# Perceiver layer on one core: context loads released by the copies of a buffer, a layer norm in 10 steps instead of 12, and re-derived instruction orders

## The reference

```
x = x + xattn(layernorm(x), context)   # second layer norm with gamma/beta, 16 heads of 64, mask over the 257 keys
x = x + attn(layernorm(x))             # self attention over the 32 tokens, 16 heads of 16
x = x + ffn(layernorm(x))              # sigmoid(xr Wr^T) * (relu(xk Wk^T)^2 Wv^T), xr/xk mix a token with the one before
```

## Time and profile before

| | us |
|---|---|
| median of 3 runs | 874.78 (873.36 to 875.11) |
| the profiled execution | 873.3 |
| span of its profile, first to last instruction | 870.3 |
| PE busy | 812.6 (93%) |
| DVE busy | 611.1 (70%) |
| ACT busy | 600.3 (69%) |
| POOL busy | 423.7 (49%) |
| mean granted TensorE clock | 0.988 of 2.4 GHz |

### The profile page before, as it was taken

How to read it: one execution, slowest core, us unless ns; L and a number is a source line. 1 busy time by engine, 2 the same in 40 slices (tenths; PEclk the granted TensorE clock), 3 DMA queues, 4 the chain that set the end, 5 groups by cost and what they waited for, 6 DMA issues and landing times.

```text
span 870.3 us, 20253 instructions
## 1 busy us (share of the span) xinstructions
PE 812.6 (93%) x7355; PEld 669.2 (77%) x7355; DVE 611.1 (70%) x1871; ACT 600.3 (69%) x1423; POOL 423.7 (49%) x664
## 2 busy tenths in 40 slices
PE   8779999999999989999999989999999989888886
PEld 7568669896788858896788868896788857677664
DVE  4744575879577884879567884879668874767375
ACT  2659876798477875799567975799567875667422
POOL 1155524665437534766337533766337534656211
PEclk9899999999999999999999999999999999999999
DMA  8311010010101020011101120110100110010000
GB/s 236 109 25 37 26 50 13 25 26 26 50 26 26 25 62 13 26 27 25 50 18 29 29 62 14 26 26 25 50 14 26 36 51 10 17 26 1 26 2 12
DMA packets 49521, 30.50 MB, mean 35 GB/s; under 512 B 22928, under 2 KB 48336, under 8 KB 49424
## 3 DMA queue, kind: packets, MB, share of 16 engines
q1 hardware_dynamic: 48528, 29.12, 12.3%
q10 hardware_dynamic: 896, 0.10, 0.1%
HBM read 26.85 MB, written 2.10 MB: 33 GB/s over the span
## 4 chain that ended last, share of the span: by engine, by line
PE 74%; DVE 12%; ACT 8%; issue 4%; SPq 1%; POOL 1%; DMA 0%; POOLq 0%; ACTq 0%; DVEq 0%
PE score L780 16%; PE pre L665 6%; PE post L866 6%; PE probT L791 5%; DVE qk_t L1281 4%; PE post L875 3%; PE aux L724 3%; PE ac_main L806 3%; PE ac_tail L808 2%; PE ac_main L807 2%; PE ac_tail L812 2%; PE ac_main L811 2%; DVE qk_l L1276 2%; PE post L846 2%; PE post L884 2%
## 5 line engine op out<-in xcount | busy, mean ns | idle before, releaser
L430 POOL TENSOR_TENSOR prT_l<-prT,prT_h 128x512 fp32r<-128x512 f32 x128 | 164.5, 1290 | 173.0 <-ACT prT_h L1070 172.8
L564 POOL TENSOR_SCALAR pr<-pr,rsum,poison 128x257 f32<-128x257 f32 x256 | 148.8, 593 | 138.0 <-DVE rsum L1305 137.0
L1299 DVE CUSTOM_DVE_ANT_0 sm<-score,mbias 128x257 f32<-128x257 f32 x256 | 106.5, 420 | 92.6 <-PE score L780 78.8
L1051 ACT ACTIVATE pr<-sm,nmx 128x257 f32<-128x257 f32 x256 | 128.8, 505 | 42.9 <-DVE nmx L1299 37.5
L780 PE MATMUL score<-cT_h,qk_h 128*128 128x258 f32 x256 | 91.6, 358 | 6.2 <-DVE qk_t L1281 4.7
L1059 ACT ACTIVATE prT<-probT 128x512 f32<-128x512 f32 x128 | 75.6, 591 | 30.0 <-PE probT L791 28.2
L791 PE MATMUL probT<-ident,pr 128*128 128x128 f32 x512 | 78.8, 277 | 9.3 <-ACT prT L1059 7.0
L1070 ACT ACTIVATE prT_h<-prT 128x512 fp32r<-128x512 f32 x128 | 80.2, 627 | 8.2 <-PE ac_tail L812 7.4
L791 PEld LDWEIGHTS probT<-ident,pr 128*128 128x128 f32 x512 | 60.3, 142 | 19.5 <-issue 7.1
L780 PE MATMUL score<-cT_h,qk_t 128*128 128x258 f32 x256 | 73.7, 288 | 0.0
L780 PE MATMUL score<-cT_h,qk_l 128*128 128x258 f32 x256 | 73.4, 287 | 0.0
(11 more groups left out here) (336 smaller groups left out, 2195.6 us busy)
## 6 DMA issues: line engine op xcount, KB each, us to landing
cx_in<-in_ctx_dram SPq DMA_DIRECT2D x64, 192.0 KB, 2.4
cx_in<-in_ctx_dram SPq DMA_DIRECT2D x64, 64.0 KB, 2.3
xn<-in_x_dram SPq DMA_DIRECT2D x8, 256.0 KB, 3.2
xb<-in_x_dram SPq DMA_DIRECT2D x8, 256.0 KB, 3.3
out_dram<-yo SPq DMA_DIRECT2D x7, 256.0 KB, 3.0
wq<-in_L_xattn_Wq_dram SPq DMA_DIRECT2D x2, 512.0 KB, 7.8
wo<-in_L_xattn_Wo_dram SPq DMA_DIRECT2D x1, 1024.0 KB, 8.2
wqkv<-in_L_attn_W_qkv_dram SPq DMA_DIRECT2D x1, 768.0 KB, 8.7
```

What stands on the lines that cost most here:

```text
L430: eng.tensor_tensor(prT_l[:, :, cut], prT[:, :, cut], prT_h[:, :, cut], ALU.subtract).then_inc(prob_lower, 1)
L564: last = pool.tensor_scalar(p, p, rsum[:, j % 2, t:t + 1], poison[:, 0:1], ALU.mult, ALU.mult)
L1051: act.activation(pr[j % 2][:, t, :], sm[:, t % 2, :], ACT.Exp, bias=nmx[:, j % 2, t:t + 1], scale=-1.0, accum_out=ssum[:, j % 2, t:t + 1]) ...
L1299: dve.tensor_tensor_reduce(sm[:, t % 2, :], score[t % 2][:, 0:NK], mbias[:], DH ** -0.5, BIG, ALU.add, ALU.min, nmx[:, j % 2, t:t + 1]).th ...
```

## The change

1. SP waits for `c_lower` (DVE's `CL`, which itself comes after ACT's `CU`, which comes after PE's `CT`) before it loads a buffer anew, and no longer for `ac_done`. In group 0 `spread_last_values()` comes behind the loads of batches 4 and 5 instead of ahead of them.
2. The layer norm has 10 steps. The seed is taken straight from the bits of the negative w by one instruction, so the shift step is gone; the polynomial of the first round is of a higher order (steps 4, 5, 6), followed by one round (7, 8), in which w2 = -1.6875 (scale var + shift) stands for w; step 9 applies. The integer tile `li` is gone.
3. The lists: the names for steps 10 and 11 of `A`, `B` and `C` are dropped in `DVE_ORDER` and `DVE_LAST`. In `DVE_FIRST`, besides, `S2:1 S3:1` go behind `A3` to `A8`, `CL:1` and `R0:1`, and `A9`, now the application, comes before `R1:1`. In `ACT_FIRST`, `P0:3` moves behind `CT:5 S1:4 S2:4 CU:4`, and `U0:7 P1:7` swap. The lists of PE and POOL are as they were.

```
-RSQRT_SEED = float(0x5F3759DF)
-NEWTON = 3
+RSQRT_SEED = float(0x5F3759DF - (1 << 30) - (1 << 22))
...
 ACT_FIRST
-    "... S0:4 CU:3 XT P0:3 CT:5 S1:4 S2:4 CU:4 U0:3 AC:2 ... CU:7 P0:7 K7 AC:6 U0:7 P1:7 K8 ..."
+    "... S0:4 CU:3 XT CT:5 S1:4 S2:4 CU:4 P0:3 U0:3 AC:2 ... CU:7 P0:7 K7 AC:6 P1:7 U0:7 K8 ..."
 DVE_FIRST
-    "... A0 A1 A2 CT:2 S2:1 S3:1 A3 A4 A5 A6 A7 CL:1 A8 R0:1 S0:2 S1:2 A9 R1:1 S2:2 S3:2 R0:2 A10 CT:3 S0:3 R1:2 S1:3 A11 R0:3 ..."
+    "... A0 A1 A2 CT:2 A3 A4 A5 A6 A7 CL:1 A8 R0:1 S2:1 S3:1 S0:2 S1:2 A9 R1:1 S2:2 S3:2 R0:2 CT:3 S0:3 R1:2 S1:3 R0:3 ..."
 DVE_ORDER
-    "... R0:1 A9 A10 S2:1 A11 WO1 B0 S3:1 ... R1:1 B9 CL:2 B10 B11 S0:2 ... C8 C9 C10 R1:5 C11 S2:6 ..."
+    "... R0:1 A9 S2:1 WO1 B0 S3:1 ... R1:1 B9 CL:2 S0:2 ... C8 C9 R1:5 S2:6 ..."
 DVE_LAST (the steps 10 and 11 dropped in the same way)
...
-                else:
-                    spread_last_values()
                 for j in range(GB if has_pre else GB - NCTX):
-                    sp.wait_ge(ac_done, g * GB + j + 1)
+                    sp.wait_ge(c_lower, g * GB + j + 1)
                     load_ctx(g * GB + j + NCTX, j % NCTX)
+                    if g == 0 and j == 1:
+                        spread_last_values()
...
                 elif stage == 2:
                     dve.tensor_scalar(w[:, own], mv[:, n, own, 1], -0.5 * scale, -0.5 * shift, ALU.mult, ALU.add)
-                    last = dve.tensor_scalar(lw[:, n, 3, own], mv[:, n, own, 1], scale, shift, ALU.mult, ALU.add)
+                    last = dve.tensor_scalar(w2[:, own], mv[:, n, own, 1], -1.6875 * scale, -1.6875 * shift, ALU.mult, ALU.add)
                 elif stage == 3:
-                    last = dve.tensor_scalar(li[:, n, own], lw[:, n, 3, own].bitcast(I32), 1, None, ALU.logical_shift_right)
-                elif stage == 4:
-                    last = dve.tensor_scalar(y[:, own].bitcast(I32), li[:, n, own], -1.0, RSQRT_SEED, ALU.mult, ALU.add)
+                    last = dve.tensor_scalar(y[:, own].bitcast(I32), w[:, own].bitcast(I32), -0.5, RSQRT_SEED, ALU.mult, ALU.add)
...
-                elif stage % 2:
+                elif stage in (4, 7):
+                    by = w if stage == 4 else w2
                     for a in part:
                         one = slice(a, a + 1)
-                        last = dve.scalar_tensor_tensor(out=q[:, one], in0=y[:, one], scalar=w[:, one], in1=y[:, one],
+                        last = dve.scalar_tensor_tensor(out=q[:, one], in0=y[:, one], scalar=by[:, one], in1=y[:, one],
                                                         op0=ALU.mult, op1=ALU.mult)
+                elif stage == 5:
+                    last = dve.scalar_tensor_tensor(out=q[:, own], in0=q[:, own], scalar=5.0 / 3.0, in1=q[:, own], op0=ALU.add, op1=ALU.mult)
                 else:
-                    last = dve.scalar_tensor_tensor(out=y[:, own], in0=q[:, own], scalar=1.5, in1=y[:, own], op0=ALU.add, op1=ALU.mult)
+                    last = dve.scalar_tensor_tensor(out=y[:, own], in0=q[:, own], scalar=1.25 if stage == 6 else 2.25, in1=y[:, own],
+                                                    op0=ALU.add, op1=ALU.mult)
```

More of the change, by code:

```diff
@@ L83 @@
     "S3:1 P1:0 U1:0 CT:3 S0:2 S1:2 P0:1 S2:2 P1:1 S3:2 AC:0 U0:1 S0:3 U1:1 S1:3 P0:2 S2:3 S3:3 CT:4 CU:2 U0:2 AC:1 P1:2 "
[1 row of a table removed]
[1 row of a table added]
     "F1 CU:5 S0:6 CT:7 S1:6 P1:4 U1:4 S2:6 S3:6 P0:5 Q2 U0:5 P1:5 AC:4 S0:7 F2 CU:6 S1:7 S2:7 Q3 K0 U1:5 S3:7 P0:6 K1 K2 "
-    "U0:6 K3 P1:6 K4 U1:6 AC:5 K5 K6 CU:7 P0:7 K7 AC:6 U0:7 P1:7 K8 U1:7 K9 CT:0 K10 K11 AC:7").split()
+    "U0:6 K3 P1:6 K4 U1:6 AC:5 K5 K6 CU:7 P0:7 K7 AC:6 P1:7 U0:7 K8 U1:7 K9 CT:0 K10 K11 AC:7").split()
 ACT_ORDER = (
@@ L100 @@
 DVE_FIRST = (
[4 rows of a table removed]
-    "CT:0 K10 K11 AC:7").split()
-DVE_ORDER = (
[5 rows of a table removed]
-    "AC:7").split()
[4 rows of a table added]
+    "AC:7").split()
+DVE_ORDER = (
[4 rows of a table added]
+    "S3:7 SG0 R1:6 SG1 FV CL:7 AC:5 K0 R0:7 K1 R1:7 K2 K3 LT K4 K5 K6 K7 AC:6 CT:0 K8 K9 K10 K11 AC:7").split()
 DVE_LAST = (
     "S0:0 S1:0 CL:0 S2:0 S3:0 R0:0 CT:1 R1:0 S0:1 S1:1 WO0 S2:1 R0:1 WO1 CT:2 B0 S3:1 B1 B2 R1:1 B3 S0:2 B4 B5 B6 B7 B8 "
[6 rows of a table removed]
-    "C9.1 C10.1 C11.1 M1.0 M1.1 FR.0 FR.1 SG.0 SG.1 FV.0 FV.1").split()
[5 rows of a table added]
+    "C4.0 C3.1 C5.0 C6.0 C4.1 C7.0 C5.1 C8.0 C6.1 C9.0 C7.1 C8.1 C9.1 M1.0 M1.1 FR.0 FR.1 SG.0 SG.1 FV.0 FV.1").split()
 POOL_FIRST = (
@@ L142 @@
 PRE = ("XT", "Q0", "Q1", "Q2", "Q3")
-FOR_PRE = PRE + tuple(f"A{n}" for n in range(6 + 2 * NEWTON)) + tuple(f"K{n}" for n in range(N_QK))
+LN_STAGES = 10
+LN_LINKS = LN_STAGES - 1
+FOR_PRE = PRE + tuple(f"A{n}" for n in range(LN_STAGES)) + tuple(f"K{n}" for n in range(N_QK))
 OF_BATCH = ("CU", "CL", "U0", "U1", "L0", "L1", "CT", "S0", "S1", "S2", "S3", "R0", "R1", "N0", "N1", "P0", "P1", "AC")
@@ L154 @@
 LOWER_ON_DVE = ("CL",)
-LN_LINKS = 5 + 2 * NEWTON
-LN_STAGES = LN_LINKS + 1
 def perceiver_layer(nc, x, ctx_in, mask, g1, be1, Wq, Wkv, Wo, bo, g2, be2, Wqkv, bqkv, Wproj, bproj,
@@ L248, in perceiver_layer @@
         lw = sb("lw", [P, 3, 4, 2])
-        li = sb("li", [P, 3, 2], I32)
         stage = acm[:].rearrange("p h t -> p (h t)")
@@ L1227, in layer_norm @@
                 before = 0 if half == 1 else g * LN_LINKS
-                w, y, q = lw[:, n, 0], lw[:, n, 1], lw[:, n, 2]
+                w, y, q, w2 = (lw[:, n, i] for i in range(4))
                 if stage > 0:
```

## The result

The changed kernel takes 870.18 us (median of 6 runs, 869.11 to 871.98) against 874.17 us before (6 runs, 872.48 to 876.49): ratio 0.9954, 95% interval 0.9936 to 0.9973. A second measurement, beside the last experiments, gave 870.39 (12 runs) against 873.23 (23 runs), 0.9969 [0.9955, 0.9982]. Forecast were 869.4 us and 0.9939. So it is faster, by 4.0 us in the first measurement and 2.8 in the second. The forecast was 5.35: its ratio lies just inside the first interval and outside the second.

A forecast was written before the change was run, and what follows sets the result against it. In the middle groups PE's own work was taken as the bound; group 0 and the last were looser. 4.3 + 0 + 1.05 + 0 = 5.35 us, off the 874.78 us median, gave 869.4 us; range 866.6 to 872.0 us.

The forecast's parts named there:

- Loads 4 and 5 ahead of the sixteen: Group 0, SP's queue: loads before the sixteen `lvc` DMAs remove PE's 4.88 us wait at `CT:4`; 4.3 us gained.
- rival (a): Group 0: short waits bring the lower clock again, its 1.7 us paid once more; 871.1, at most 872.5 us; chance 0.17.
- the four that I had named: PE, group 0: waits of 0.7 (`U1:1`), 0.2 (POOL), 1.7 (`CT:4`'s lower part) and 0.5 us (`P0:3`).
- the walk: Group 0: three other queues followed from 56 us; of 6.6 us, 2.3 turn into waits for ACT and DVE.
- The sign that I had named for a wrong walk: Group 0: `CT:4` without a wait, yet a gain below 3 us, would show the walk through ACT's queue wrong.
- `c_lower` elsewhere: All other loads: going out up to 15 us earlier gives 0 us, as PE waits for no load in middle groups.
- Layer norm: Two steps fewer on DVE: 0.6 us at `B` in the last group, 0.45 us at closing `C.0`; 1.05 us in sum.
- Groups 1 to 6: hidden behind PE: Middle groups: the shorter norm changes nothing there; without that cover it would be worth 1.7 us a group.
- the sign that I had named for them: Middle groups: if shorter than 98.6 us, the claim that PE's own work sets them is wrong.
- The lists: Reordered lists, chiefly group 0: between -0.5 and +1 us, taken as 0.
- Rival (b): Group 0: ACT's new order and earlier `A9` take up the 2.3 us given back; 867.1 us; chance 0.17.
- Rivals (c) and (d): No change, load 4 late for another reason, 874.8 us, chance 0.04; group 0 wholly at lower clock, 883 us, 0.05.

The follow-up runs named there:

- experiment 2: Kernel before with the 10-step layer norm alone (SP's queue as before, the dropped steps' names taken out of the lists): 873.26 us, ratio 1.0006.
- experiment 3: Changed kernel with group 0's ACT and DVE lists as they were before: 870.7 us, ratio 0.997.
- experiment 4: Changed kernel with one context load of eight waiting for `ac_done` again in groups 1 to 7: 869.27 us, ratio 0.996.
- experiment 7: Changed kernel with 64 more waits at the start of DVE's program, shifting its stream by 32 records: 869.29 us, run once.
- experiment 1: Kernel before with SP's edit alone (`c_lower` for all loads, sixteen `lvc` DMAs behind loads 4 and 5): 870.76 us, ratio 0.9971.
- experiment 6: Changed kernel with eight more waits at the start of DVE's program, a shift of 4 records: single executions from 865.34 to 871.81 us.
- shifts of 64 and 128: Changed kernel with 128 or 256 more waits at DVE's start, shifting its stream by 64 or 128 records: 875.31 and 884.76 us, run once each.
- experiment 11: Kernel before with only the sixteen `lvc` DMAs moved behind loads 4 and 5, `ac_done` kept: 874.39 us, ratio 1.0022.
- experiment 5: Changed kernel with `AC:0 S2:3` ahead of `R0:3` in DVE's list of group 0: 869.87 us, ratio 0.9972.
- both mends: Changed kernel with eight more waits at DVE's start and `AC:0 S2:3` ahead of `R0:3` in group 0: 867.38 us, ratio 0.9935.

## Why the prediction was right, and where not

**Loads 4 and 5 ahead of the sixteen (forecast 4.3 us).** The cause was named rightly: without the edit of SP's queue group 0 gains nothing (experiment 2: 0.15 us lost), with it 2.3 to 4.2. The size 4.3 nearly holds in the executions at full clock: 4.19, 3.93 and 3.86 us in experiments 3, 4 and 7. In four others (the changed kernel twice, experiments 1 and 6) it is 2.28, 2.36, 2.46 and 2.25; the kernels with shifts of 64 and 128, with their late start, gained 2.34 and 2.28, also at the lower clock. The difference, about 1.7 us, is rival (a), at just its price: the lower clock comes back behind a short wait. I gave it 0.17; four of these seven profiles show it, six of nine with the other two. The mis-sized term is thus this one: 3.0 us as the mean of the seven, and not 4.3. The waits were not the four that I had named. The largest, `CT:4`'s lower part at 1.7 us, was not there; its place took 1.9 us at `AC:1`, which the walk missed because it followed the context and the exponents but not the second thing that `weigh` waits for, `act_copied` of the batch before, queued on DVE behind `R0:3`. The sign that I had named for a wrong walk came: `CT:4` has no wait, and group 0 gains less than 3 us.

**`c_lower` elsewhere (0).** Right for the middle: 98.6 us a group in experiment 1. But to price it apart from the order of the sixteen was wrong for group 0: alone, the order makes group 0 2.8 us longer (experiment 11).

**Layer norm.** `B` 0.6 forecast, 0.56 measured; `C.0` 0.45 and 0.47, with PE's wait at 2.28 us for 2.3. The step that failed is "Groups 1 to 6: hidden behind PE". The arithmetic was hidden as said (DVE's busy time fell by 11.2 us, for 13 forecast); the instruction count was not. The 9 instructions that fall away in a group set the count at 256, and the 128-record place then falls on the one mask behind which PE's bank is freed: 1.75 us lost, more than the 1.05 us that the part was to give. By itself this part is worth nothing (1.0006). That is also why the groups are not the 98.6 us forecast; the sign that I had named for them was shorter groups, not longer ones.

**The lists (0).** Right as far as the noise of 1.75 us lets one see: 870.7 with the old ones, in a set where the kernel before was 872.66, a ratio of 0.997 as that of the changed kernel measured again.

**The sum.** 5.35 us were forecast. The parts as measured give 3.0 + 1.0 - 1.75 = 2.3 us, and the two comparisons 4.0 and 2.8. The number came out close (869.4 for 870.2) by luck in part, because the median that it starts from, 874.78 of 3 runs, was high: later sets of 23 and 30 runs gave 872.4 to 873.2. Rival (b) was not seen in the changed kernel; what it asked for, a better order, came with experiment 5. Rivals (c) and (d) are excluded by the measured time.

**What stays open.** Why the clock falls behind the same wait in six executions and not in three; experiment 5 and both mends, with the wait nearly gone, show full clock in their one profile each, which is too little to call it cured. And why the 128-record place costs time: the runs show where it comes, what it costs and that an instruction packet comes with it, not what DVE does there. The Trainium skill, Runtime: NRT & Kernel Launch, section Instruction fetch mechanics, tells of an engine's program being refilled in blocks of 16 KiB (256 instructions) and calls the cost of crossing one "mostly hidden". That something happens at a fixed count of the stream agrees with these runs. The size does not: here packets are 8 KB, the place comes every 128 records, and 0.36 us of it were not hidden.

## What to carry to other kernels

A long issue in a queue is a block with two neighbours: when it is moved, ask at what time it will now start and which load stands behind it. When a stop is taken away, walk every semaphore that the next instructions wait for, the free-buffer ones too; and look whether the waits that remain are long enough to bring the lower clock. When a change removes instructions from a periodic stream and a period gets longer by the same few tenths each time, put a few idle instructions ahead of the loop before believing any theory about the neighbours, and look at when the packets of the instruction queue start.

## What the runs showed of the hardware that was not expected

- DVE's stream has a place every 128 records (703, 831, 959, 1087 ...) where an instruction that DVE waits to start comes 0.36 us late. It was seen at the masks `S2:7` and, with 0.19 us, at one wait of the kernel before. With a period of 256 records it hits the same job each time.
- Instruction packets of 8 KB start within 1.2 us of these late masks, and 128 more records bring one more packet.
- An issue of SP that runs while a DVE mask is released does not delay it: 0.10 to 0.11 us from the wait instruction to the mask in five groups of experiment 1.
- Behind the same wait of 1.9 us at `AC:1`, kernels that differ elsewhere run that stretch of group 0 at a clock of 1.00 or at 0.76 to 0.85 (mean of 63 to 70 us), 1.7 us apart; single executions of the kernel with a shift of 4 reach from 865.34 to 871.81 us.
